# Channel variances packed as 128 rows by 64 columns instead of 64 rows by 128 columns

## The reference

```
x = x + L1(_gn(x))                        # 4 images
for d in (rows, columns):                 # two sequences of 65536 pixels, 64 channels
    fx  = (x - mean_c) / sqrt(var_c + eps) * g + b      # layer norm over the 64 channels
    h   = 2 Re(C xs) + D fx,  xs = scan forward and backward of B fx
    x2  = gelu(h) + fx
    fx2 = layer norm of x2 over the 64 channels
    y_d = fx2 @ enc.T @ dec.T + fx2
out = W_fusion @ concat(y_rows, y_columns) + bias
```

## Time and profile before

| | |
|---|---|
| time, median of 3 runs | 9992.77 us (9988.87 to 9994.73) |
| span of the profiled execution, first to last instruction | 9990.8 us |
| what the median has beside that span | 2.0 us |
| busy: PE, PEld, DVE, ACT, POOL | 9274.8, 6465.7, 8185.9, 6225.9, 1663.5 us |
| mean granted TensorE clock | 0.970 |
| one input half, from its first L1367 to the first L1758 | 1497.5 to 1694.3 us, 196.7 us |
| one output half, to the next pass's first L1367 | 1694.3 to 2091.8 us, 397.5 us |

### The profile page before, as it was taken

One profiled execution on the slowest core, in us unless ns is written; L12 is line 12 of the kernel. 1 busy time (PEld: TensorE's weight loads), 2 busy tenths in 40 slices (PEclk: granted clock), 3 DMA queues, 4 the chain that ended last, 5 costly groups with the idle time before them and its releaser, 6 DMA issues.

```text
span 9990.8 us, 185091 instructions
## 1 busy us (share of the span) xinstructions
PE 9274.8 (93%) x71718; PEld 6465.7 (65%) x71718; DVE 8185.9 (82%) x11975; ACT 6225.9 (62%) x10071; POOL 1663.5 (17%) x1824
## 2 busy tenths in 40 slices
PE   1899998999899998998989999899998999989998
PEld 1677765656577775565667777565566777746565
DVE  7788888888688887988868888887986888888786
ACT  0566656566666665556766666655676666665666
POOL 0000002333300000333320000133341000023334
PEclk9999999999999999999999999999999999989999
DMA  3677767575677676658567767756666666674755
GB/s 104 150 147 143 144 126 233 177 244 159 158 150 147 142 144 160 204 173 252 160 152 147 147 142 143 208 166 196 209 181 125 134 131 128 122 240 155 232 175 157
DMA packets 1333108, 1650.89 MB, mean 165 GB/s; under 512 B 845180, under 2 KB 1077260, under 8 KB 1246988
## 3 DMA queue, kind: packets, MB, share of 16 engines
q1 hardware_dynamic: 1332236, 1639.05, 65.1%
HBM read 785.79 MB, written 514.86 MB: 130 GB/s over the span
## 4 chain that ended last, share of the span: by engine, by line
PE 80%; DVE 11%; issue 4%; ACT 3%; DMA 1%; SPq 1%; POOL 0%; DVEq 0%; ACTq 0%; POOLq 0%
PE ps L822 15%; PE ps L1758 14%; PE ps L1771 7%; PE ps L789 6%; PE ps L1782 5%; PE ps L780 5%; PE ps L836 4%; PE ps L1408 3%; PE ps L855 3%; PE ps L880 3%; PE ps L867 3%; PE ps L816 2%; PE ps L883 2%; PE ps L796 2%; DVE S L1542 2%
## 5 line engine op out<-in xcount | busy, mean ns | idle before, releaser
L1151 DVE SCALAR_TENSOR_TENSOR F<-U,LW,F 106x512 f32<-106x512 f32 x2048 | 1536.1, 750 | 54.5
L1758 PE MATMUL ps<-fp,Dwr 128*128 128x512 f32 x6144 | 1549.0, 401 | 1.8 <-DVE tt L1528 1.8
L1758 PEld LDWEIGHTS ps<-fp,Dwr 128*128 128x128 f32 x6144 | 1114.9, 188 | 618.4 <-ACT x L1847 290.5
L1129 DVE TENSOR_TENSOR Z<-ps,LW 128x340 f32<-128x340 f32 x1024 | 522.9, 511 | 745.1 <-PE ps L789 725.5
L1847 ACT ACTIVATE x<-ps,cst 128x512 f32<-128x512 f32 x512 | 351.8, 687 | 1039.9 <-PE ps L1771 1035.6
L822 PE MATMUL ps<-P,WP 128*128 128x512 f32 x3072 | 905.0, 417 | 31.6 <-DMA H<-P 31.6
L822 PE MATMUL ps<-H,WP 128*128 128x512 f32 x3072 | 916.9, 420 | 0.0
L949 ACT ACTIVATE XF<-ps 128x340 f32<-128x340 f32 x1024 | 466.4, 455 | 684.3 <-PE ps L780 683.6
L1771 PE MATMUL ps<-XP,Cwr 128*128 128x512 f32 x3072 | 807.1, 399 | 82.6 <-DVE XP L1893 82.6
L789 PE MATMUL ps<-XF,Rfwd 128*128 128x340 f32 x2048 | 799.2, 472 | 21.0 <-ACT XF L949 20.6
L1069 POOL TENSOR_SCALAR xo<-xo 64x512 f32<-64x512 f32 x4 | 6.0, 1499 | 4839.9 <-DVE xo L1185 4839.9
(11 more groups left out here) (301 smaller groups left out, 19378.7 us busy)
## 6 DMA issues: line engine op xcount, KB each, us to landing
H<-P SPq DMA_DIRECT2D x512, 585.0 KB, 7.2
raw<-x SPq DMA_DIRECT2D x240, 640.0 KB, 11.5
fx_d<-fx SPq DMA_DIRECT2D x112, 1024.0 KB, 6.5
fl_d<-fp SPq DMA_DIRECT2D x112, 1024.0 KB, 6.9
fp<-fl_d SPq DMA_DIRECT2D x112, 1024.0 KB, 6.6
fx<-fx_d SPq DMA_DIRECT2D x112, 1024.0 KB, 5.4
x1h_d<-xo SPq DMA_DIRECT2D x256, 256.0 KB, 9.0
x1v_d<-xo SPq DMA_DIRECT2D x512, 128.0 KB, 8.0
```

The lines of the kernel that those rows point to most:

```text
L1129: e.tensor_tensor(Z[t % 2][:, 2 * c:2 * c + 2, :].rearrange("p a b -> p (a b)"), ps[6][:, 0:2 * HID], Wt, ALU.mult).then_inc(sem["z"], 1)
L1151: ins = e.scalar_tensor_tensor(o, u, wd[0:106, i:i + 1], o, ALU.mult, ALU.add)
L1758: ins = e.matmul(bank(m)[:], Dwr[:, w, c:c + 128], fq[n % 2][x][:, s2, :], start=(s2 == 0 and w == 0 and x == 0), stop=False)
```

## The change

`variances` writes 32 different rows in each quadrant and 64 columns, in place of 16 different rows and 128 columns: block q is cut in two (h = 0, 1), each with its own picker, so a group has 32 matmuls over 64 columns in place of 16 over 128. All later operations on `rs` and `rh` have 64 columns in place of 128. `RD` keeps its 512 columns, now as eight blocks of 64 with an 8-column `own_q`: in the input half ScalarE issues eight activations of 64 columns in place of four of 128, in the output half VectorE's L1329 keeps its size. `En` grows by 132 columns, so that all tiles behind it move up by as many bytes; 512 bytes are left free behind `rh`.

```diff
-                e[par * 64:par * 64 + 64, i, r] = 1.0 / 64
-                for q in range(4):
-                    b[q, r, i, q, par * 64:par * 64 + 64] = 1.0
+                for h in range(2):
+                    e[par * 64:par * 64 + 64, h, i, 16 * h + r] = 1.0 / 64
+                b[:, r, i, par * 64:par * 64 + 64] = 1.0
                 mask[:, r] = -c
...
-    En, Bc = at("En", [128, 133]), at("Bc", [128, 1024], F32R)
-    lows, own_q = En[:, 128:129], En[:, 129:133]
+    En, Bc = at("En", [128, 265]), at("Bc", [128, 1024], F32R)
+    lows, own_q = En[:, 256:257], En[:, 257:265]
...
-    rs = at("rs", [128, 128])
-    rh = at("rh", [128, 128], F32R)
+    rs = at("rs", [128, 64])
+    rh = at("rh", [128, 64], F32R)
+    offset[0] += 512
...
-        e.tensor_tensor(RD[:].rearrange("k (q c) -> k q c", q=4), rs[:].unsqueeze(1).to_broadcast([128, 4, 128]),
-                        own_q.unsqueeze(2).to_broadcast([128, 4, 128]), ALU.mult).then_inc(sem[out], 1)
+        e.tensor_tensor(RD[:].rearrange("k (q c) -> k q c", q=8), rs[:].unsqueeze(1).to_broadcast([128, 8, 64]),
+                        own_q.unsqueeze(2).to_broadcast([128, 8, 64]), ALU.mult).then_inc(sem[out], 1)
 
     def variances(e, o, i, src, pick):
-        for q in range(4):
-            ins = e.matmul(o[32 * q:32 * q + 32, 0:128], pick[:, 32 * i:32 * i + 32], src[:, 128 * q:128 * q + 128],
-                           start=(i == 0), stop=(i == 3))
+        for h in range(2):
+            for q in range(4):
+                c = 128 * q + 64 * h
+                ins = e.matmul(o[32 * q:32 * q + 32, 0:64], pick[:, 128 * h + 32 * i:128 * h + 32 * i + 32], src[:, c:c + 64],
+                               start=(i == 0 and h == 0), stop=(i == 3 and h == 1))
         return ins
...
-            for q in range(4):
-                ins = e.activation(RD[:, 128 * q:128 * q + 128], rs[:], ACT.Identity, scale=own_q[:, q:q + 1])
+            for q in range(8):
+                ins = e.activation(RD[:, 64 * q:64 * q + 64], rs[:], ACT.Identity, scale=own_q[:, q:q + 1])
             ins.then_inc(sem["rd"], 1)
...
-                e.activation(rs[:], ps[2][:, 0:128], ACT.Sqrt, bias=eps[:]).then_inc(sem["sd"], 1)
+                e.activation(rs[:], ps[2][:, 0:64], ACT.Sqrt, bias=eps[:]).then_inc(sem["sd"], 1)
...
-                e.activation(rs[:], ps[4][:, 0:128], ACT.Sqrt, bias=eps[:]).then_inc(sem["se"], 1)
+                e.activation(rs[:], ps[4][:, 0:64], ACT.Sqrt, bias=eps[:]).then_inc(sem["se"], 1)
```

More of the change, by code:

```diff
@@ L90, in constants @@
     k["k_ctr"] = (p[:, None] // 64 == p[None, :] // 64) * ((p[:, None] == p[None, :]) - 1.0 / 64)
-    e = np.zeros((128, 4, 32))
-    b = np.zeros((4, 32, 4, 4, 128))
-    mask = np.zeros((4, 32, 1))
+    e = np.zeros((128, 2, 4, 32))
+    b = np.zeros((8, 16, 4, 128))
+    mask = np.zeros((8, 16, 1))
     for par in range(2):
@@ L97, in constants @@
                 r = 4 * i + 2 * c + par
-                e[par * 64:par * 64 + 64, i, r] = 1.0 / 64
-                for q in range(4):
-                    b[q, r, i, q, par * 64:par * 64 + 64] = 1.0
+                for h in range(2):
+                    e[par * 64:par * 64 + 64, h, i, 16 * h + r] = 1.0 / 64
+                b[:, r, i, par * 64:par * 64 + 64] = 1.0
                 mask[:, r] = -c
-    k["k_E"] = np.concatenate([e.reshape(128, 128), mask.reshape(128, 1), np.kron(np.eye(4), np.ones((32, 1)))], 1)
-    k["k_Bc"] = np.concatenate([b.sum(3).reshape(128, 512), np.roll(b.sum(3), 64, 3).reshape(128, 512)], 1)
+    k["k_E"] = np.concatenate([e.reshape(128, 256), mask.reshape(128, 1), np.kron(np.eye(8), np.ones((16, 1)))], 1)
+    k["k_Bc"] = np.concatenate([b.reshape(128, 512), np.roll(b, 64, 3).reshape(128, 512)], 1)
     k["k_id"] = 1.0 * (p[:, None] % 64 == np.arange(64)[None, :])
```

## The result

| | before | after |
|---|---|---|
| median | 9993.68 us (4 runs) | 10040.67 us (4 runs, 10040.02 to 10044.48) |
| span of the profiled execution | 9990.8 us | 10038.5 us |
| ratio after / before | | 1.005, 95% interval 1.0036 to 1.0064 |

The kernel became 0.5% slower; 10039 us was predicted. By stretches of the two profiled executions: the eight input halves (first centring to the first L1758, L1761 after) take 1613.4 us in place of 1570.2, +43.2; the eight output halves, to their last reciprocal, +1.4; what precedes the first input half, +3.1 (1497.5 against 1500.6); the rest, layer 0 for the next image among it, nothing.

A forecast was written before the change was run, and what follows sets the result against it. TensorE was taken to bound the output half, and a loop through TensorE, ScalarE and `norm` to cap VectorE's relief in the input half. 43.7 + 2.1 + 3.0 - 4.4 + 1.5 = 45.9 us gave 10039 us, range 10015 to 10065.

The forecast's parts named there:

- VectorE's small operations: Reciprocal, rounding and low part on 64 fewer columns: 0.50 us less a group, counting at most 0.08 in the input half.
- 0.08 a round: Input half: how late VectorE's queue is at `norm` after TensorE's broadcast; all that a quicker VectorE can win.
- The spread: ScalarE's `RD` in the input half, eight pieces for four: 2.02 us against 1.28, 0.74 more a group.
- The round: Input half: later `RD` moves `norm` and all behind it by +0.42 us, in 104 rounds 43.7 us.
- The variances: TensorE's burst of 16 rounds of 64 columns: +0.02 us a group in 256 groups, 2.1 and 3.0 us.
- stand in line: Rival, chance 0.09: the variances' weight loads do not pipeline, +0.88 us in each burst, 10259 us.
- The tails: Ends of halves: output 0.55 us shorter each, 4.4 less in all; input +0.19 each, 1.5 more.
- the second loop: Input half: centring on TensorE, ScalarE's copies and `RD`, TensorE's broadcast, then `norm`; only 0.24 us to spare at `RD`.

## Why the prediction was right

Point by point, with what the profile or a run shows:

- **VectorE's small operations**, 0.50 us less: 0.40 for the reciprocal, 0.07 for L1321 (0.05 predicted), 0.03 for the rounding (226 to 194 ns; 0.05 predicted): 0.50. That it counts for only 0.08 a round was the decisive reading; with that part alone the kernel won 18 us, not 60.
- **The spread**, 2.02 us predicted, 2.02 measured. The pieces start 0.24 us apart. This one term, run alone, gives the whole loss (+46.8 us against +47.0).
- **The round**: +0.42 and +0.02 predicted; reciprocals stand 11.58 us apart against 11.16, +0.42 in all. Where I wrote 0.62 from broadcast to `norm`, from one round, the mean is 0.635, which takes 0.015 off. VectorE idles 1.00 us in the round shown, where about 0.9 was predicted: 0.50 saved, 0.42 waited, and the 0.08 by which it is no longer late.
- **The variances**, +0.02 a burst: 1.10 against 1.08, and +0.02 in every group of the output half. Loads of 110 ns do not keep rounds of 64 columns from following each other at half the former distance. The Trainium skill ("TensorE: Matmul & The Clock Gate", The mechanism) says in one sentence that a load overlaps with matmuls in flight only when its row group differs, and would have had them stand in line; 64 records in 1.10 us disagree with that. Another sentence of the same section names a second case, a load into a background weight buffer, and that one they do not contradict.
- **The tails**: TensorE's wait at the end of an output half was 3.76 us and is 3.20, -0.56 for -0.55. At the end of an input half the sum was wrong. The way from root to broadcast grew by 0.09 us (4.54 to 4.63) where +0.19 was given, but what follows was left out: before the change `norm` stands there in VectorE's queue behind the two rotations, 0.94 us after the broadcast, and after it 0.54. So from reciprocal to `norm` the way became shorter, 3.90 to 3.72 us, and eight tails give 1.4 us back in place of costing 1.5. Below, before:

```profile
1680.28 2.47 DVE L1528 SCALAR_TENSOR_TENSOR tt<-ps,cst,TBi 128x1024 f32<-128x1024 f32 x2
1681.73 0.73 PE L1389 MATMUL ps<-RD,Bc 128*128 128x512 f32 x2 [1.68 <-ACT RD L1467]
1682.67 2.03 DVE L1504 TENSOR_TENSOR fx<-ps,xc 128x512 f32<-128x512 f32 x3
```

And after:

```profile
1691.54 0.73 PE L1392 MATMUL ps<-RD,Bc 128*128 128x512 f32 x2 [1.75 <-ACT RD L1470]
1692.08 1.29 DVE L1507 TENSOR_TENSOR fx<-ps,xc 128x512 f32<-128x512 f32 x2 [0.26 <-PE ps L1392]
```

That the total, 47 us, lies within 2 us of the forecast is partly luck. On the spans it is 47.7 against 45.9. The input halves came out 43.2 against 47.8 (43.7 + 2.1 + 0.5 for their other 24 groups + 1.5), 4.6 less, and 2.9 of that is the tail just told. Two things made up for it. One is the 3.1 us ahead of the first input half, which go with the granted clock and differ between executions. The other is the rest of the span, +1.4 where 2.6 - 4.4 = -1.8 was given. The four output halves that lead straight into another input half did as forecast (-1.0 together against -0.9), so that difference lies in the stretches with layer 0 or in the last output half, and no cause is shown for it. The mechanism and its size are shown; the agreement to 2 us is not.

## What to carry to other kernels

A stage in which one engine is 99% busy need not be bound by that engine alone: before taking work from it, measure in one round how late it is at the hand-over where it meets the second loop (here 0.08 us), since that is all the relief can buy until the other loop is shortened too. Cutting columns in half saves the engine whose cost goes by the column (the reciprocal, 6.2 ns each) and costs the one with a fixed price for every instruction (ScalarE: pieces of 128 columns start 0.29 us apart, those of 64 still 0.24, so 64 columns cost 0.05 and some 0.19 is fixed). A change that loses for such a reason is worth keeping in hand: once the spread and the order of the broadcasts had been mended, the same edit was worth 52 to 55 us.

## What was not expected of the hardware

The narrow matmuls of the variances follow each other at the rate of their streamed columns: 16 rounds of 64 columns in four quadrants take 1.10 us, 8 rounds of 128 columns 1.08, though every load takes 110 ns. With two tiles in place of four it is the same, 16 rounds of 64 columns in 1.09. And half of `RD`, 128 x 256 out of two broadcast operands, costs GpSimd 0.62 us, in a gap where it had nothing to do, against 0.96 us that ScalarE needs for four more pieces (2.02 less 1.06).
